# A four-layer graph network on one core: the first stage in another order

## The reference, cut to what matters

```
edge_index = [src, dst]                            # 8192 edges, dst sorted; 512 nodes, 512 features
h = relu(layernorm(x));  z = layernorm(h) * ln1_g + ln1_b
q, k, v = z@Wq + bq, z@Wk + bk, z@Wv + bv          # 8 heads of 64
scores = q[src] . k[dst] / 8 + edge_attr           # an edge's bias per head
p = exp(scores - m[src]);  alpha = p / segment_sum(p, src)[src]
att = segment_sum(alpha * v[dst], src) @ Wo + bo
... feed-forward part, then three more layers (SAGE, GCN, GIN), each x = x + layer(relu(layernorm(x)))
```

## Time and profile before

| | us |
|---|---|
| median of 3 runs | 404.5 (404.4 to 405.52) |
| the profiled execution's own time | 406.24 |
| its span | 404.8 |
| busy: PE, DVE, ACT | 373.0, 308.9, 168.8 |
| first `pairs` of group 0 starts | 33.62 |
| last `pairs` (group 20) ends, on the chain that ended last | 118.91 |

### The profile page before, as it was taken

How to read it: one execution, slowest core, us unless ns; L and a number is a source line. 1 busy time by engine, 2 the same in 40 slices (tenths; PEclk the granted TensorE clock), 3 DMA queues, 4 the chain that set the end, 5 groups by cost and what they waited for, 6 DMA issues and landing times.

```text
span 404.8 us, 5033 instructions
## 1 busy us (share of the span) xinstructions
PE 373.0 (92%) x1764; PEld 278.6 (69%) x1764; DVE 308.9 (76%) x659; ACT 168.8 (42%) x281; POOL 5.3 (1%) x25
## 2 busy tenths in 40 slices
PE   2597689999999999999989999999999999999994
PEld 1363245566666788887858788887678878787773
DVE  5848878999947788998795978499875777597346
ACT  4452476764103333335565923342363531135310
POOL 5000000000000000000000000000000000000000
PEclk9999899999999999999999999999999999999989
DMA  7500255543115300026800050500230032000002
GB/s 245 231 1 2 66 163 170 180 146 107 63 44 148 113 2 2 0 74 215 336 0 2 5 202 2 207 0 2 88 122 0 0 115 96 0 2 0 0 2 104
DMA packets 16360, 32.92 MB, mean 81 GB/s; under 512 B 1360, under 2 KB 1488, under 8 KB 16336
## 3 DMA queue, kind: packets, MB, share of 16 engines
q1 hardware_dynamic: 15744, 32.25, 23.1%
q10 hardware_dynamic: 592, 0.36, 0.3%
HBM read 21.07 MB, written 1.05 MB: 55 GB/s over the span
## 4 chain that ended last, share of the span: by engine, by line
PE 71%; DVE 16%; ACT 5%; issue 4%; DMA 3%; SPq 1%; ACTq 0%; DVEq 0%
PE acc L1481 8%; PE bank L1463 8%; PE bank L1575 7%; PE bank L1337 6%; PE bank L1338 6%; PE bank L1318 4%; PE acc L1318 4%; PE acc L1337 4%; PE acc L1338 4%; PE bank L1560 3%; PE acc L1546 3%; DVE big_rounded L674 2%; PE acc L1295 2%; PE bank L1295 2%; PE acc L1640 2%
## 5 line engine op out<-in xcount | busy, mean ns | idle before, releaser
L1481 PE MATMUL acc<-wide_rounded,c_rounded 128*126 128x512 f32 x168 | 51.8, 444 | 9.1 <-ACT acc L510 7.4
L1481 PEld LDWEIGHTS acc<-wide_rounded,c_rounded 128*126 128x126 f32 x168 | 30.7, 188 | 28.0 <-issue 22.8
L814 DVE TENSOR_SCALAR wide_rounded<-iota_f,picked 128x512 fp32r<-128x512 f32 x84 | 36.9, 482 | 7.6 <-PE acc L1481 7.6
L505 ACT COPY z_sb<-acc 126x512 f32<-126x512 f32 x37 | 21.6, 585 | 45.0 <-PE acc L1481 23.9
L529 ACT ACTIVATE wide<-wide,low_col 128x512 f32<-128x512 f32 x32 | 21.3, 716 | 32.9 <-DVE low_col L972 32.8
L1575 PEld LDWEIGHTS bank<-v_sb,big 128*128 128x128 f32 x256 | 29.7, 192 | 4.7 <-issue 4.0
L647 DVE TENSOR_TENSOR wslot_rounded<-wslot,wide_rounded 128x512 fp32r<-128x512 f32 x24 | 16.2, 688 | 21.2 <-ACT wslot L415 21.2
L1575 PE MATMUL bank<-v_sb,big 128*128 128x65 f32 x256 | 31.6, 277 | 0.0
L1463 PE MATMUL bank<-t_sb,wslot 128*128 128x512 f32 x64 | 30.9, 608 | 0.4 <-DVE t_sb L903 0.4
L674 DVE TENSOR_TENSOR big_rounded<-big,big_rounded 128x1024 fp32r<-128x1024 f32 x24 | 29.1, 1222 | 0.5
L820 DVE TENSOR_TENSOR c_rounded<-row_bc,wslot_rounded 128x1008 fp32r<-128x1008 bf16 x21 | 25.3, 1202 | 0.1
(11 more groups left out here) (338 smaller groups left out, 777.1 us busy)
## 6 DMA issues: line engine op xcount, KB each, us to landing
big<-z_sb SPq DMA_DIRECT2D x36, 252.0 KB
big<-in_w SPq DMA_DIRECT2D x4, 2048.0 KB, 7.9
x_sb<-in_x SPq DMA_DIRECT2D x8, 256.0 KB, 4.8
big<-in_w_3t SPq DMA_DIRECT2D x2, 1024.0 KB, 7.4
row_bc<-in_rows SPq DMA_DIRECT2D x7, 256.0 KB, 6.5
wslot<-in_wq SPq DMA_DIRECT2D x1, 1024.0 KB, 8.4
wslot<-in_wk SPq DMA_DIRECT2D x1, 1024.0 KB, 10.3
wslot<-in_wv SPq DMA_DIRECT2D x1, 1024.0 KB, 12.3
```

The costliest lines, as they stand in the source:

```text
L505: nc.scalar.copy(stage[0:BROWS, b % STAGES, :], a).then_inc(S["staged"], 1)
L814: nc.vector.tensor_scalar(hot_ring[:, u, k, :], iota_f[:, :], picked[:, 0, s0 + k:s0 + k + 1], None, ALU.is_equal)
L1481: last = nc.tensor.matmul(to, st_ring[:, u, 2 * k + a, :, :].rearrange("p w k -> p (w k)"), hot_ring[:, u, k, :], start=False, stop=False, ...
```

## The change

All of it lies in the first stage, before and in the groups. On DVE: `bmax` is reduced before `x_moments(2)`; the copy of `src`, the second reduction and `ln_coefs(0)` come before the counts; the moments of h stand elsewhere among the slot tables; `bmax_all` and `ln_coefs(1)`, `ln_plain` come before `slot_columns`; the four one-hots of group 0 stand before the `t_sb` copies; the block ends' numbers (`ends_u`, the trip count) and the one-hots of group 1 come before the weights. On PE: the transposed `bmax` goes to bank 3 and is made early; `keep_warm` matmuls (128x512 bf16, results unused) are put at five places, 12 in all, where there were 4 at one place; z is transposed into banks 6, 7, 4, 5 in place of 0 to 3, so `first_weights` no longer waits for the copies, while the transposes now wait for `slot_columns`; the first `choices` comes after the six early QKV steps. The 38 steps are dealt as three for groups 0 to 8, two for group 9 and one for groups 10 to 18.

```diff
-        qkv_group = [-1] * EARLY + [g for g, steps in enumerate([2] * (NG - 2) + [0, 0]) for _ in range(steps)]
+        qkv_group = [-1] * EARLY + [g for g, steps in enumerate([3] * 9 + [2] + [1] * 9 + [0, 0]) for _ in range(steps)]
...
         LAST_V = range(3 * NT - 2, 3 * NT)
+        Z_BANKS = (6, 7, 4, 5)
...
                 act.wait_ge(S["turned"], t + 1)
-                nc.scalar.activation(t_sb[:, t, :], bank[t][:, :], ACT.Identity, bias=colp("ln1_b", t),
+                nc.scalar.activation(t_sb[:, t, :], bank[Z_BANKS[t]][:, :], ACT.Identity, bias=colp("ln1_b", t),
...
             by_two = in_whole.rearrange("p (h a) s -> p h a s", a=2)
+            dve.wait_ge(S["bias_in"], 16)
+            nc.vector.tensor_reduce(bmax[:, 0:HP], att_b, AX.X, ALU.max).then_inc(S["bias_top"], 1)
...
             x_moments(3)
+            dve.wait_ge(S["src_in"], 16)
+            mark(nc.vector.tensor_copy(src_f, idx_src))
+            dve.wait_ge(S["bias_turned"], 1)
+            nc.vector.tensor_reduce(top_c[:, :], bank[3][0:HP, P:2 * P].rearrange("p (a t) -> p a t", a=2), AX.X,
+                                    ALU.max).then_inc(S["bias_column"], 1)
+            ln_coefs(0)
...
             nc.vector.tensor_tensor(count, bank[4][0:NBK, SPAN:SPAN + 1], flag, ALU.add).then_inc(S["counts_ready"], 1)
-            ln_coefs(0)
-            dve.wait_ge(S["src_in"], 16)
-            mark(nc.vector.tensor_copy(src_f, idx_src))
-            dve.wait_ge(S["bias_in"], 16)
-            nc.vector.tensor_reduce(bmax[:, 0:HP], att_b, AX.X, ALU.max).then_inc(S["bias_top"], 1)
+            dve.wait_ge(S["h_ready"], 1)
+            moments(0, h_sb, "ln_var")
...
             slot_table(0, 0, whole)
-            dve.wait_ge(S["h_ready"], 1)
-            moments(0, h_sb, "ln_var")
-            slot_picks(0, whole)
...
                 moments(t, h_sb, "ln_var")
-            dve.wait_ge(S["bias_turned"], 1)
-            nc.vector.tensor_reduce(top_c[:, :], bank[6][0:HP, P:2 * P].rearrange("p (a t) -> p a t", a=2), AX.X,
-                                    ALU.max).then_inc(S["bias_column"], 1)
+            slot_picks(0, whole)
...
             moments(3, h_sb, "ln_var")
-            slot_columns(0, 1, whole)
+            dve.wait_ge(S["bias_spread"], 1)
+            nc.vector.tensor_scalar(bmax_all[:, 0:HP], bank[3][:, 0:HP], -1.0, W_SHIFT, ALU.mult, ALU.add
+                                    ).then_inc(S["bias_low"], 1)
...
                 ln_plain(1, t, h_sb)
-            dve.wait_ge(S["bias_spread"], 1)
-            nc.vector.tensor_scalar(bmax_all[:, 0:HP], bank[6][:, 0:HP], -1.0, W_SHIFT, ALU.mult, ALU.add
-                                    ).then_inc(S["bias_low"], 1)
+            slot_columns(0, 1, whole)
...
             dve.wait_ge(S["tables"], 13 + NT)
-            one_hots(0, 0, (0, 1))
+            one_hots(0, 0)
...
                 dve.wait_ge(S["turned"], t + 1)
-                nc.vector.tensor_scalar(t_sb[:, t, :], bank[t][:, :], colp("ln1_g", t), colp("ln1_b", t),
+                nc.vector.tensor_scalar(t_sb[:, t, :], bank[Z_BANKS[t]][:, :], colp("ln1_g", t), colp("ln1_b", t),
                                         ALU.mult, ALU.add).then_inc(S["t_vector"], 1)
-            one_hots(0, 0, (2, 3))
-            dve.wait_ge(S["weights_mm"], 1)
-            dve.wait_ge(S["w_whole"], 1)
-            nc.vector.copy_predicated(by_two, with_second(whole, HP, 2), from_tables(1)).then_inc(S["w_mixed"], 1)
-            dve.wait_ge(S["w_mixed"], 1)
-            dve.sem_inc(S["weights_read"], 1)
-            rounded(4, early, by_two[:, :, :, early])
-            left_sides(0, 0)
-            one_hots(1, GROUP)
-            dve.wait_ge(S["w_hi"], 1)
-            step(7, nc.vector.tensor_tensor(wp[:, later, 1, 0:H], in_whole[:, :, later].rearrange("p h s -> p s h"),
-                                            wp[:, later, 0, 0:H].bitcast(F32), ALU.subtract))
-            left_sides(1, GROUP)
-            step(8, slot_masks(next_masks))
...
                                            ).then_inc(S["ends_ready"], 1)
+            one_hots(1, GROUP)
+            dve.wait_ge(S["weights_mm"], 1)
+            dve.wait_ge(S["w_whole"], 1)
+            by_two = in_whole.rearrange("p (h a) s -> p h a s", a=2)
+            nc.vector.copy_predicated(by_two, with_second(whole, HP, 2), from_tables(1)).then_inc(S["w_mixed"], 1)
+            dve.wait_ge(S["w_mixed"], 1)
+            dve.sem_inc(S["weights_read"], 1)
+            rounded(4, early, by_two[:, :, :, early])
+            left_sides(0, 0)
+            dve.wait_ge(S["w_hi"], 1)
+            step(7, nc.vector.tensor_tensor(wp[:, later, 1, 0:H], in_whole[:, :, later].rearrange("p h s -> p s h"),
+                                            wp[:, later, 0, 0:H].bitcast(F32), ALU.subtract))
+            left_sides(1, GROUP)
+            step(8, slot_masks(next_masks))
...
             nc.tensor.matmul(bank[4][0:ET, NBK:2 * NBK], downto, meets, start=True, stop=True).then_inc(S["ranks_mm"], 1)
+            keep_warm(7, 1)
+            pe.wait_ge(S["bias_top"], 1)
+            nc.tensor.transpose(bank[3][0:HP, P:2 * P], bmax[:, 0:HP], ident[:, :]).then_inc(S["bias_turned"], 1)
...
                              ).then_inc(S["outer_mm"], 1)
+            keep_warm(7, 3)
...
-            def bias_turned():
-
-                pe.wait_ge(S["bias_top"], 1)
-                nc.tensor.transpose(bank[6][0:HP, P:2 * P], bmax[:, 0:HP], ident[:, :]).then_inc(S["bias_turned"], 1)
-
...
                 for a in range(2):
-                    last = nc.tensor.matmul(bank[6][a * ET:(a + 1) * ET, 0:HP],
+                    last = nc.tensor.matmul(bank[3][a * ET:(a + 1) * ET, 0:HP],
...
                 for h in range(HP):
-                    pe.wait_ge(*((S["t_vector"], h + 1) if h < 2 else (S["t_ready"], 2 * h - 2)))
...
                     pe.wait_ge(*((S["t_vector"], k + 1) if k < 2 else (S["t_ready"], 2 * k - 2)))
+                if n == 1 and k == 0:
+                    pe.wait_ge(S["t_vector"], 2)
...
             all_slots = slice(0, SLOTS)
-            bias_turned()
+            bias_spread()
+            keep_warm(7, 2)
             slot_tables(0, all_slots)
+            keep_warm(7, 2)
             slot_edges(0, all_slots)
-            bias_spread()
+            keep_warm(7, 4)
             pe.wait_ge(S["rows_ready"], 1)
-            held = choices(0, 2 * GROUP)
-            keep_warm(7, 4)
+            pe.wait_ge(S["round_steps"], 3)
...
                 for c in range(NT):
-                    last = nc.tensor.transpose(tile(bank[c], t), tile(z_sb[:, t, :], c), ident[:, :])
+                    last = nc.tensor.transpose(tile(bank[Z_BANKS[c]], t), tile(z_sb[:, t, :], c), ident[:, :])
...
                         last.then_inc(S["turned"], 1)
-            pe.wait_ge(S["bias_low"], 1)
...
                 qkv_step(i)
+            held = choices(0, 2 * GROUP)
...
                 pairs(g, g % RING, held[GROUP * (g % 2):GROUP * (g % 2 + 1)])
-                if g == 0:
-                    pe.wait_ge(S["round_steps"], 3)
```

## The result

The changed kernel takes **393.31 us** (393.01 to 394.19, 4 runs) where the kernel before takes 404.45 (403.79 to 405.52, 4 runs): 11.1 us less, ratio 0.9726, 95% interval 0.9699 to 0.9752. The forecast was 392.9, with a range from 390.5 to 397.5. The profiled execution has a span of 391.6 us.

A forecast was written before the change was run, and what follows sets the result against it. PE, 92% busy, was taken as the bound, with idle time to remove. Stage end 30.75 + 71.7 + 3.0 + 1.4 + 0.4 = 107.3, not 118.9; so 404.5 - 11.6 = 392.9 us, range 390.5 to 397.5.

The forecast's parts named there:

- Counts' chain: DVE in the setup: five small instructions moved ahead of L861 make it 0.5 us later (bounds 0 and 1.0).
- Reciprocal: DVE in the setup: the second norm's reciprocal comes at 17.4 instead of 18.92, 1.5 us earlier.
- Transposes: PE in the setup: the transposes of z, gated by `slot_columns`, start at 19.6 instead of 21.35.
- The fast rate of the transposes: PE before group 0: 16 transposes of z take 2.0 us, not 3.62, so `t_sb` starts at 21.6.
- the slow rate: PE before group 0: the transposes stay at 3.62 us; `t_sb` about 22.7, 1.75 us earlier than before.
- The first copy: ACT at the block ends: first copy at about 31.4 instead of 39.6, block 3's at 40.5.
- PE's wait: PE in the early groups: idles 1.8 us, then two waits of about 0.6; idle time 3.0 us.
- 1.4 for DVE: Late groups: DVE's building and taking out of two V products cost PE 1.4 us (between 0.7 and 3.5).
- 0.4 for the loads: PE's register loads after groups 11, 13, 15 and 17 cost 0.1 us each (bounds 0 and 4.2).
- this rival: Clock: slow transposes (+1.1) or a fall after 1.8 us idleness (about 1.7): 394.0 to 395.7 us; chance 0.12.
- the slower case: Ten register loads each stop PE for 1.92 us, not hidden behind queued steps: 412.1 us; chance 0.02.
- waited for its bank: Group 4: product 5's first step waits for product 3's bank; PE loses 2 us: 394.9 us; chance 0.05.

The follow-up runs named there:

- a_no_warm: Changed kernel without the eight added `keep_warm` matmuls (the four ahead of the transposes stay): 393.63 us, ratio 0.9719 to the kernel before.
- b_ends_early: Kernel before with only the four statements making the block ends' numbers moved early, behind `one_hots(0, 0, (2, 3))`: 400.38 us, ratio 0.9885.
- b_dealt: Kernel before with only the new deal of QKV steps: 400.53 us, ratio 0.9897.
- a_ends_late: Changed kernel with the block ends' numbers made last again: 397.14 us, ratio 0.9816 to the kernel before.
- a_even: Changed kernel with the QKV steps dealt as before, two for each of 19 groups: 397.92 us, ratio 0.9830 to the kernel before.
- a_order_alone: Changed kernel with steps dealt as before and block ends' numbers made last: 401.78 us, ratio 0.9929 to the kernel before.

## Why the prediction was right

**Start.** Counts' chain: forecast 0.5 later, measured 0.6. `slot_picks`: 15.0, measured 14.86. Reciprocal: 17.4, measured 17.25. Transposes: 19.6, measured 19.46. Up to here all within 0.15 us. Two things went otherwise inside. The bias landed at 6.25, so `bmax` was reduced there and delayed the x moments by 0.45 us, more than the 0.3 that I had as the worst. And the small instructions ahead of L861 lay in the wait for ACT's square root.

**The fast rate of the transposes was the step that failed.** I took 2.0 us and laid it to the added `keep_warm`. The profile had 3.09, `t_sb` at 22.34 and not 21.6, group 0 at 31.46 and not 30.75; and a_no_warm shows that the added matmuls are not what sets it. Had I taken the slow rate as the sum's term, group 0 would have been at 31.85. The term belongs into the range, not into the sum. The slow end was not firm either: the 3.62 us were read from one execution, and the same transposes took 2.83 and 2.40 in b_ends_early and b_dealt.

**Block ends.** The first copy came at 32.31 (forecast 31.4), 0.9 late, 0.7 of it from group 0's start; block 3's 9.10 behind it (9.1). PE's wait was 1.70 us (1.8), with the later ones 2.5 in all (3.0). The shape was right: a_ends_late and b_ends_early move these copies by themselves and cost 3.8 and gain 4.1.

**Waits and late groups, two terms off by opposite amounts.** By content (1.86 a group, 0.86 a step), PE should go from 31.46 to the start of group 10 in 10 x 1.86 + 29 x 0.86 = 43.5 us; it came there at 78.70, after 47.2. So the waits cost 3.7 us, not 3.0. Idle time before `pairs` is 2.5 of it. Each of the three starts from rest costs 0.26 more (two matmuls take 0.72 us behind a wait, 0.46 in the chain; four take 1.19 and 0.93), together 0.8. And 0.35 is a change of view: the timeline has group 0 start at 31.46, the chain, from which 78.70 is read, at 31.81. The forecast, which adds to a start read from the timeline, had no term for these two. From 78.70 to 107.38 it took 28.7 us for 11 x 1.86 + 9 x 0.86 = 28.2: 0.5 us in place of the 1.4 for DVE and 0.4 for the loads. DVE was not the bound, though nearly: from 79.20 to 105.03 it had no idle time, built a group in 2.70 us (PE's 2.72, and 2.8 that I had) and took out two V products of 0.6 us between. But it had a lead: groups 12 to 19 were each built 1.0 to 1.9 us before PE came to them, group 20 about 0.3. That lead, which the term left out, took up the products. The timeline of DVE, from the one-hots of one group to those of the next:

```profile
85.42 1.67 DVE L815 TENSOR_SCALAR wide_rounded<-iota_f,picked 128x512 fp32r<-128x512 f32 x4
87.01 1.20 DVE L821 TENSOR_TENSOR c_rounded<-row_bc,wslot_rounded 128x1008 fp32r<-128x1008 bf16 x1
88.13 1.66 DVE L815 TENSOR_SCALAR wide_rounded<-iota_f,picked 128x512 fp32r<-128x512 f32 x4
```

So the sum hit 107.3 against 107.38 because +0.7 at the start, +0.7 in the waits and -1.3 in the late groups cancel. The mechanism was right; that the end fits to 0.1 us is luck.

**Rivals.** In the changed kernel's profile the granted clock is 1.00 from group 0 to group 20, as forecast. But it did fall after a wait in other executions (2.71 us in a_even, 1.66 in a_no_warm), so this rival deserved more than 0.12. In a_no_warm the groups took 0.9 us more than in the changed kernel, with a stretch at half clock among them; I had 1.7; its idle time before `pairs` was 0.4 us less. The register loads were not exposed (0.20 us at most), and loads moved ahead of the steps cost 3.1 us, far from the 17 of the slower case. No step waited for its bank: the three steps behind group 4, the last of them product 5's first, ran in 2.74 us (from 54.65) without a gap. Four 128x512 bf16 matmuls took 1.89 us at 17.69 and 1.03 at 30.78, and the granted clock fell to 0.50 behind idle stretches. The clock rule of the Trainium skill (TensorE: Matmul & The Clock Gate, "The HAM clock gate") has the same direction: half clock by default, full clock after sustained work, half again after idleness. How the idle stretches of these profiles compare is in the last section.

## What to carry to other kernels

When the first of a ring of buffers is released late, find who makes the numbers that the releasing engine needs. Moving four tiny instructions ahead of the weights gained 4.1 us by the medians, the whole new order of the setup 2.3, though their intervals overlap. Give the engine that is the bound more of its independent work ahead of a wait whose length is a DMA's, and less later, where another engine's pace leaves room. Check parts one at a time: here they added up, but a part that looked sensible (warming matmuls) was worth nothing that can be told. And compare the same instructions between several profiles before you read a gain from one: here 16 transposes differed by 1.1 us and the end of the kernel by 1.6 us with no edit to them.

## What was not expected of the hardware

The granted clock fell behind some waits of PE and not behind others of the same length. It fell 1 to 3 us behind the end of waits of 3.06 us (before), 2.62 (a_ends_late), 2.22 (b_dealt), 1.66 (a_no_warm) and 1.44 (a_order_alone), and within those of 2.71 (a_even) and 2.63 us (b_ends_early). It did not behind 2.62 us before 50.13 in the kernel before, 2.55 in a_order_alone and 1.70 in the changed kernel. In a_no_warm:

```profile
44.00:46.00 2.00, 2.00 (x5) 0.61 0.74 236
46.00:48.00 2.00, 2.00 (x4) 0.53 0.47 152
```

Block 0 leaves in four DMAs of 36 KB, and the last of them lands 6.20 us after its issue has begun (35.13 above). Block 4, 252 KB in one DMA, needs 3.51, counted in the same way:

```profile
43.16 3.51 DMA big<-z_sb
```

Size doesn't order them. The share of the 16 DMA engines does differ. The first row below holds the end of block 0's transfer, the second the DMAs of block 4 and later ones (granted clock, DMA share and GB/s are the last three numbers):

```profile
40.00:42.00 2.00, 1.15 (x4) 1.00 0.13 36
...
44.00:46.00 2.00, 2.00 (x7) 1.00 0.66 211
```

A share of 0.13 is that of two engines out of 16 (an estimate), and each of the four DMAs writes two nodes' rows of `big`, where the others write fourteen. Whether that is the reason was not tried; a run with block 0 sent in another shape would be the test.

And what lies behind the stage has two lengths 1.6 us apart, whichever kernel runs, by a stretch at half clock while PE is busy. It was there in six of fourteen profiles, each time 260 to 280 us behind the stage's end.
